# Attention softmax maxima: the copy out of PSUM moves from VectorE to ScalarE, the splitting to GpSimd

## The reference

```python
q = apply_rope(q); k = apply_rope(k)
attn = jnp.einsum('bqhd,bkhd->bhqk', q, k) * scale
attn = jnp.where(mask[None, None], -1000000000.0, attn)   # causal
attn = jax.nn.softmax(attn, axis=-1)
out = jnp.einsum('bhqk,bkhd->bqhd', attn, v).reshape(B, S, D)
```

## Time and profile before

| | |
|---|---|
| runs | 892.44, 892.99, 894.50 us, median 892.99 |
| profiled execution | 890.49 us, its span 888.7 us |
| granted TensorE clock, mean | 0.985 |
| attention stages 0 to 15 | about 127 to 545 us of the span |
| TensorE, VectorE, ScalarE, GpSimd busy | 94%, 67%, 56%, 37% of the span |

### The profile page before, as it was taken

The page is one execution under the profiler, slowest core; times in us unless marked ns, Lnnn a source line. Parts: engine busy times, 40 slices in busy tenths (PEclk is TensorE's granted clock), DMA queues, the critical chain, the costliest instruction groups (busy, mean ns, idle before and its releaser), DMA issues. The chain is left out here.

```text
span 888.7 us, 24625 instructions
## 1 busy us (share of the span) xinstructions
PE 835.6 (94%) x8767; PEld 524.4 (59%) x8768; DVE 597.9 (67%) x1133; ACT 497.6 (56%) x1168; POOL 327.6 (37%) x469
## 2 busy tenths in 40 slices
PE   6999859999989999999999988789999999999995
PEld 4555433444434444434444434569999999999994
DVE  4888999898878898988888902966433333333331
ACT  4668426777767777777877795024333333333330
POOL 9999663343233434324243431634111111111111
PEclk9999988999999999999999999999999999999998
DMA  8578632553433333322333323968555555555540
GB/s 280 156 234 260 180 110 77 175 169 87 107 87 87 98 87 99 81 79 72 89 92 96 113 41 101 294 236 256 199 182 178 177 177 178 182 183 178 177 173 0
DMA packets 62643, 129.50 MB, mean 146 GB/s; under 512 B 16217, under 2 KB 43482, under 8 KB 56282
## 3 DMA queue, kind: packets, MB, share of 16 engines
q1 hardware_dynamic: 58282, 112.99, 42.4%
q0 software_dynamic: 4272, 15.29, 4.7%
HBM read 100.35 MB, written 23.44 MB: 139 GB/s over the span
## 5 line engine op out<-in xcount | busy, mean ns | idle before, releaser
L891 ACT ACTIVATE arena<-ps_pair 128x512 f32<-128x512 f32 (+2 forms) x640 | 308.6, 565 | 99.9 <-PE ps_pair L1214 96.7
L971 DVE TENSOR_REDUCE B_block_max<-ps_item 128x8 f32<-128x1024 f32 x288 | 338.1, 1220 | 32.4 <-PE ps_item L1118 31.4
L1214 PE MATMUL ps_pair<-q_stack,k_stack 99*32 99x512 bf16 (+7 forms) x3072 | 191.5, 333 | 9.2 <-ACT arena L891 5.5
L805 POOL TENSOR_SCALAR_AFFINE_SELECT arena<-arena 128x256 f32<-128x256 f32 x256 | 102.9, 408 | 164.5 <-ACT arena L891 160.3
L1214 PEld LDWEIGHTS ps_pair<-q_stack,k_stack 99*32 99x32 bf16 (+1 forms) x3072 | 79.0, 96 | 134.0 <-ACT arena L891 88.6
L1231 PE MATMUL ps_pair<-arena,B_v_quad 128*32 128x512 f32 (+3 forms) x1536 | 153.9, 494 | 1.2 <-ACT B_oacc L910 0.5
L1855 PEld LDWEIGHTS C_bank<-arena 128*128 128x128 f32 x1248 | 146.1, 193 | 1.9
L1855 PE MATMUL C_bank<-arena 128*128 128x128 f32 x1248 | 146.4, 276 | 0.0
L1875 PE MATMUL C_ps_p<-arena 128*128 x624 | 141.0, 379 | 0.0
L1875 PEld LDWEIGHTS C_ps_p<-arena 128*128 128x128 f32 x624 | 115.6, 190 | 14.1
L1507 ACT ACTIVATE arena<-C_bank,ffn_columns 128x128 f32<-128x128 f32 x156 | 44.5, 368 | 141.7 <-PE C_bank L1855 141.7
(11 more groups left out here) (168 smaller groups left out, 672.6 us busy)
## 6 DMA issues: line engine op xcount, KB each, us to landing
arena<-in_w_exp SPq DMA_DIRECT2D x41, 1024.0 KB, 5.0
qk_parts<-arena SPq DMA_DIRECT2D x32, 384.0 KB, 3.4
q_stack<-qk_parts SPq DMA_DIRECT2D x96, 128.0 KB, 3.0
k_stack<-qk_parts SPq DMA_DIRECT2D x64, 128.0 KB, 3.0
arena<-in_w_exp POOLq DMA_DIRECT2D x6, 1024.0 KB, 6.9
rows<-payload SPq DMA_DIRECT2D x39, 130.5 KB, 2.1
arena<-in_x SPq DMA_DIRECT2D x8, 512.0 KB, 5.1
arena<-in_x_feat SPq DMA_DIRECT2D x8, 512.0 KB, 6.1
```

Source lines behind the costliest of these rows:

```text
L805: pool.affine_select(out=block_p, in_=block_p, compare_op=ALU.is_ge, fill=0.0, base=0, pattern=[[0, 2], [1, P]], channel_multiplier=-1).th ...
L891: act.activation(pr[s % PR][:, h:h + 2 * n - 1:2, 0:W], ps_s[(EXPS * Q.const + exps_to[s] + u) % R][:, 0:n * W].rearrange("p (h n) -> p h ...
L971: dve.tensor_reduce(bmx[:, g:QH:GH, first:first + 3 * gap + 1:gap], src[:, :, :].rearrange("p c (b n) -> p c b n", n=P), AX.X, ALU.max).th ...
L1214: mm = pe.matmul(bank[at:at + 32, :], ks[rows, r, half, bass.ds(g * SEQ + kb * P + at, 32)], qs[rows, r, half, bass.ds(g * SEQ + c * QW + ...
```

## The change

ScalarE copies the transposed maxima out of PSUM, negated, into a new float32 tile `ng` (line 930 of the changed kernel). It does so behind the first exponential of the stage's second block; in stage 0 ahead of everything. GpSimd then forms all three parts in six steps, the two of VectorE among them (a cast, a product, a sum, and the three as before). VectorE handles items only. The maxima's buffer is now freed by ScalarE, so that readings are counted by two semaphores, `s_free` for items and `s_mt` for the maxima, and TensorE waits on both where it waited on one.

```diff
+        ng = sb("B_negated_maxima", [MAXR, P])
+        s_mt = sem("B_max_rows_negated")
+        NEG_AT = 1
-        def wait_free(eng, i, item, alone=None):
-            wait(eng, s_free, i, ITEMS, number(i, item) + 1, alone)
+        def freed_by(i, back):
+            order = [e[1] for m in range(-1, i.const + 1) for e in plan_of(Step(m)) if present(Step(m), e[1]) is not None]
+            upto = ITEMS * i.const + number(i, back[0]) + 1 - back[1]
+            return sum(item != MAXT for item in order[:max(0, upto)]), sum(item == MAXT for item in order[:max(0, upto)])
+        def wait_free(eng, i, item, back=0):
+            items, maxima = freed_by(i, (item, back))
+            if items > 0:
+                eng.wait_ge(s_free, items)
+            if maxima > 0:
+                eng.wait_ge(s_mt, maxima)
...
-                            wait_free(pool, i, MAXT)
+                            wait(pool, s_mt, i, 1, 1)
                             wait(pool, s_row, i, 32, 0)
+                            pool.tensor_copy(n0[:, :], ng[:, :]).then_inc(s_n2, 1)
+                            wait(pool, s_n2, i, 5, 1)
+                            pool.tensor_tensor(n2[:, :], n0[:, :], cst[0:MAXR, C_REST:C_REST + 1].to_broadcast([MAXR, P]),
+                                               ALU.mult).then_inc(s_n2, 1)
+                            wait(pool, s_n2, i, 5, 2)
+                            pool.tensor_tensor(nr[:, :], n2[:, :], ng[:, :], ALU.add).then_inc(s_n2, 1)
+                            wait(pool, s_n2, i, 5, 3)
                             pool.tensor_copy(n1[:, :], nr[:, :]).then_inc(s_n2, 1)
...
+                    if i.const == 0:
+                        negate(i)
...
                         for u in range(exps[s]):
+                            if i.within(NQ) and k == NEG_AT and u == 1 and i.const > 0:
+                                negate(i)
...
+                def negate(i):
+                    wait_full(act, i, MAXT)
+                    wait(act, s_n3, i, 1, 0)
+                    act.activation(ng[:, :], buffer(i, MAXT)[0:MAXR, 0, 0:P], ACT.Copy, scale=-1.0).then_inc(s_mt, 1)
...
-                    wait_full(dve, i, item)
-                    if item == MAXT:
-                        wait(dve, s_n3, i, 1, 0)
-                        dve.tensor_scalar(n0[:, :], src[0:MAXR, 0, 0:P], -1.0, None, ALU.mult).then_inc(s_n1, 1)
-                        wait(dve, s_n1, i, 1, 1)
-                        dve.scalar_tensor_tensor(out=nr[:, :], in0=n0[:, :], scalar=cst[0:MAXR, C_REST:C_REST + 1], in1=src[0:MAXR, 0, 0:P],
-                                                 op0=ALU.mult, op1=ALU.subtract).then_inc(s_free, 1)
+                    if item != MAXT:
+                        wait_full(dve, i, item)
...
-                        wait(pe, s_free, i, ITEMS, number(i, item) - 1)
+                        wait_free(pe, i, item, 2)
```

More of the change, by code:

```diff
@@ L787, in emit @@
                         if k == NM_AT and i.within(NQ):
-                            wait_free(pool, i, MAXT)
+                            wait(pool, s_mt, i, 1, 1)
                             wait(pool, s_row, i, 32, 0)
+                            pool.tensor_copy(n0[:, :], ng[:, :]).then_inc(s_n2, 1)
[5 more added lines that the diff above has]
+                            wait(pool, s_n2, i, 5, 3)
                             pool.tensor_copy(n1[:, :], nr[:, :]).then_inc(s_n2, 1)
-                            wait(pool, s_n2, i, 2, 1)
+                            wait(pool, s_n2, i, 5, 4)
                             pool.tensor_tensor(n2[:, :], n1[:, :], cst[0:MAXR, C_REST + 1:C_REST + 2].to_broadcast([MAXR, P]),
                                                ALU.mult).then_inc(s_n2, 1)
-                            wait(pool, s_n2, i, 2, 2)
+                            wait(pool, s_n2, i, 5, 5)
                             pool.tensor_tensor(nm[:, :], n2[:, :], nr[:, :], ALU.add).then_inc(s_n3, 1)
@@ L958, in reduce_item @@
                     src = buffer(i, item)
-                    wait_full(dve, i, item)
-                    if item == MAXT:
-                        wait(dve, s_n3, i, 1, 0)
-                        dve.tensor_scalar(n0[:, :], src[0:MAXR, 0, 0:P], -1.0, None, ALU.mult).then_inc(s_n1, 1)
-                        wait(dve, s_n1, i, 1, 1)
-                        dve.scalar_tensor_tensor(out=nr[:, :], in0=n0[:, :], scalar=cst[0:MAXR, C_REST:C_REST + 1], in1=src[0:MAXR, 0, 0:P],
-                                                 op0=ALU.mult, op1=ALU.subtract).then_inc(s_free, 1)
-                    else:
+                    if item != MAXT:
+                        wait_full(dve, i, item)
+                    if item != MAXT:
                         b, g = place(item)
@@ L1098, in put_item @@
                         if ahead(i, item):
-                            wait(pe, s_free, i, ITEMS, number(i, item))
+                            wait_free(pe, i, item, 1)
                         else:
-                            wait(pe, s_free, i, ITEMS, number(i, item) - 1)
+                            wait_free(pe, i, item, 2)
                         b, g = place(item)
```

## The result

The changed kernel takes 902.79 us (median of 4 runs, 902.36 to 904.35), the kernel before 892.72 us beside it (889.25 to 894.5). The medians differ by 10.1 us. The forecast was 893.7, with 896.1 as the upper end. The profiled executions are further apart than the medians (904.35 against 890.49 us, spans of 902.6 and 888.7), so a stage-by-stage account of the traces has to explain 13.9 us, and some of that is scatter.

What follows compares the result with a forecast made beforehand. Each stage was taken to be paced by TensorE's row of instructions; VectorE 0, copy 0.2, buffer 0.5, extra waits 0 and GpSimd 0 summed to +0.7 us, giving 893.7 us, with a range of 891.8 to 896.1.

Steps and rivals of the forecast that it cites:

- GpSimd's part: +1.37 us a stage, 0 on the path: GpSimd's chain forming the parts: three more steps make it 1.37 us longer, but SyncE comes later anyway, so 0.
- VectorE, 0 on the path: VectorE's two maxima steps go, 0.63 us a stage, but its next reduction waits for TensorE's item: 0 gained.
- Rival 1: VectorE is the bound, so 9.5 us go: 883.5 us, chance 0.05; in half the stages 888.9, chance 0.03.
- The copy: ScalarE's added copy, 277 ns a stage: 0 on the path in 15 stages, 0.2 us in stage 15.
- The buffer that TensorE waits for: TensorE's item using the maxima's bank, now freed by ScalarE: 0.04 us late in 13 stages, +0.5 us.
- Stage 0: No earlier stage as cover: parts ready 0.5 us later, yet landing before the scores start: 0, at most 0.5 us.
- The extra waits: One wait more on TensorE at some 270 other items and transposes: 0, at most 13.7 us.
- rival 4: Longer parts chain reaches TensorE in stage 0 and where GpSimd's masks are late: 894.2 to 895.2 us, chance 0.07.

Runs made afterwards that it cites:

- experiment 12: Changed kernel with weight transfers apart, padding behind operand loads, one wait a stage, copy one exponential earlier: 900.77 us; kernel before with the first two: 900.11; kernel before: 903.19.
- Experiment 10: Changed kernel, but VectorE forms the first part and first rest from ScalarE's copy, GpSimd keeping its three old steps: 902.82 us, ratio 1.0118 to the kernel before.
- experiment 11: Changed kernel with weight transfers apart, padding behind operand loads, one wait a stage, and ScalarE's copy one exponential earlier: 888.22 against 891.12 us, ratio 0.9977.
- experiment 4: Changed kernel with TensorE waiting for the negation once a stage instead of at each item: 900.42 us, ratio 1.0076 to the kernel before.
- experiment 6: Padding transfers behind stage 4's operand loads, weight transfers apart: changed kernel, also one wait a stage, 902.27 us (0.999), again 889.8 (0.9978); kernel before 888.28 (0.9952).
- experiment 3: Kernel before with three more GpSimd steps in the 13 stages other than 1, 2 and 14: 893.9 us, ratio 1.0003.
- experiment 1: Changed kernel with GpSimd's weight transfers of stages 1, 2 and 14 issued four blocks later: 908.24 us, ratio 1.0168 to the kernel before.
- the kernel with two steps: Kernel before with two more GpSimd steps ahead of the parts' last one in stages 1, 2 and 14: 893.63 against 891.12 us, ratio 1.0022.
- experiment 9: Kernel before with three more GpSimd steps in all 16 stages, VectorE still negating: 896.77 against 891.12 us, ratio 1.0058.

## Why the prediction was wrong

**The step that failed** is "GpSimd's part: +1.37 us a stage, 0 on the path". Its size was right: the steps of stage 8 run from 344.52 to 347.12, 2.60 us against 1.28. The cover was read from plain stages alone (SyncE comes later anyway, the scores need the rows six microseconds later), and for stages 1, 2 and 14 the text looked at GpSimd's masks and not at the transfers. In the kernel before, SyncE issues the parts 4.72 us behind the transpose in stage 8, but 2.38 in stages 1 and 2, 0.03 behind the end of the chain: the cover isn't there. And two things hang on the chain's end in these stages. It releases SyncE's transfers of the parts, and the weight transfers stand behind it in GpSimd's order, so both start at the same time. And the price of a landing was taken from other transfers in other places (2.4 us, the median of 32). Landing behind two 1 MB transfers took 11.12 - 2.38 = 8.7 us already in the kernel before, with 0.26 us to spare against the scores. The last row is the very transfer that mattered, but it was read for its 1.32 us on GpSimd and not for its landing. Worked out from landings in the trace of before: 1.44 us later with margins of 0.26, 0.51 and 0.60 us in stages 1, 2 and 14 gives 1.2 + 0.9 + 0.8 = 2.9 us, a forecast of 896.6, which is still too low. The measured loss of those stages, 9.27 us, has two more terms: the landing slips by more than the issue (3.33 us for 1.44 in stage 1), and the clock falls behind a stall (1.6 us in stage 1, about 1.7 in stage 2, where 3.46 - 1.76 - 0.05 us are left). The prediction had a term for neither.

**VectorE, 0 on the path**: right. Its wait in stage 8 ahead of the reduction is now 1.52 us, as forecast 1.5:

```profile
344.33 2.36 DVE L995 TENSOR_REDUCE B_block_max<-ps_item 128x8 f32<-128x1024 f32 x2 [1.52 <-PE ps_item L1142]
```

Rival 1 is out by this row and by experiment 12. Experiment 10 adds that it is not symmetric: to be 0.69 us later on VectorE costs 0.56.

**The copy**: right. 16 copies of 273 ns in the median, against 277 from the row; the estimate by the Trainium skill (ScalarE: Activation LUTs, What ACT_TABLE_LOAD costs) was 293 ns, 20 too much. Stage 15 was given 0.2 us and got 0.1: leaving out the three traces with a fall of the clock in it, it takes 31.35 or 31.36 us with the copy where the change puts it, and 31.24 or 31.25 without the copy or with the copy one exponential earlier.

**The buffer that TensorE waits for**: right in place and size, 0.055 us a stage against 0.04, in 14 stages instead of 13 once stage 4's stall is out of the way, and gone when the copy ends earlier (experiment 11).

**Stage 0**: right. The parts leave 3.53 us behind the transpose instead of 3.01, land at 6.68, and the scores start at 7.00 as before.

**The extra waits**: right, 0 (experiment 4).

**Stage 4** had no term. On the mean of the traces it cost 1.6 us more in the changed kernels, with ranges that overlap. In the two kernels compared here it is 2.04 us: TensorE's stall for the operand loads is 3.25 us instead of 2.27, and the clock is lower around it (0.72 from 258 to 270, against 0.86 from 250 to 262 before). That the padding ahead of the loads makes the stall is shown (experiment 6); why it is longer with the change stays open.

**Of the 13.9 us between the two profiled spans**, 9.27 are stages 1, 2 and 14, 2.04 stage 4 (where the same kernel scatters by 1 to 3 us), 0.4 the other stages from 3 to 13; up to the end of stage 0 the kernel after is 0.8 us ahead. The rest can't be put down to the change: 1.45 us in stage 15 are 0.1 of the copy and a granted clock of 0.81 for 9 us, which a kernel with VectorE's negation showed too (experiment 3, 0.82) and the changed kernel of experiment 1 did not (1.00); 1.44 lie behind the attention, where the same part took 344.6 to 349.3 us in the traces of the faster sets.

**The range** was too narrow for a reason that can be named: rival 4 had the right mechanism, a longer chain that reaches TensorE, but was bounded by the masks' lateness of 0.5 to 1.5 us in all, and not by the landing of what the chain releases.

## What to carry to other kernels

When a chain gets longer, list everything that its last step releases or has queued behind it, DMA issues too, and take the landing time of each from the stage where it happens, next to what else is in flight. The margin between that landing and its user is the number that decides; here it was 0.26 to 0.60 us in three stages of sixteen, 0.84 in stage 0, and over three in the rest. In this kernel a small transfer issued together with two large ones was about as late as they were, and moving both large ones within the stage handed the delay to the next transfers; one in each stage left no wait.

## What the runs showed of the hardware

- In stage 1, two transfers of 12 KB beside two of 1 MB landed 8.7 us after the first issue in the kernel before (up to 10.6 in the kernel after), beside one of 1 MB in 6.1 (9.90 - 3.82), without them in 3.1 (6.88 - 3.82).
- The clock behind a stall of TensorE: after 2.88, 2.43, 2.23 and 2.20 us it was granted at 0.65 or 0.66 over the next 5 us, after 1.76 us at 0.72 over 4; after 1.04, 1.06, 1.44 and 1.96 us it stayed at 1.00. The stall of 1.96 us, longer than one that lost the clock, shows that its length alone doesn't decide. So do two stalls in stage 4: after 1.05 us (the kernel with two steps) the next 4 us had 0.59, after 1.69 us (experiment 9) 1.00. Two stretches of the experiment with GpSimd's part alone, behind its stalls of 2.20 and 1.96 us:

```profile
165.00:170.00 5.00, 5.00 (x64) 1.86 (x66) 2.97 (x3) 3.27 (x7) 1.18 (x3) 0.66 0.55 151
194.00:198.00 4.00, 3.95 (x72) 2.02 (x72) 2.97 (x3) 3.38 (x8) 1.22 (x3) 1.00 0.59 165
```

- Each of SyncE's padding transfers took 0.49 us to issue as a rule, and each operand load 0.6. In all fourteen traces with the padding ahead of the loads, two to four of these 23 issues took 0.9 to 2.1 us. In the six with ScalarE's copy one or two of them were padding, in the eight others none was over 0.83. No row names what held them.
